# A message phase on one core: four buffers of compared places, four PSUM banks, a later turn for every engine, and a quarter of the filter loads on GpSimd's queue

## The reference

```python
xn = node @ Wn
f = ssp(edge @ We1 + be1)
f = f @ We2 + be2
msg = xn[edge_index[1]] * f                    # the message phase
agg = jax.ops.segment_sum(msg, edge_index[0], num_segments=N)
```

## Time and profile before

| | us |
|---|---|
| median of 3 runs | 5333.97 (5328.78 to 5336.42) |
| the profiled execution, device time | 5331.8 |
| its span from the first to the last instruction | 5329.5 |
| message phase in it, 1457 to 1983 | 526 |
| per turn of the phase, 526 / 208 | 2.53 |

### The profile page before, as it was taken

How to read it: one execution, slowest core, us unless ns; L and a number is a source line. 1 busy time by engine, 2 the same in 40 slices (tenths; PEclk the granted TensorE clock), 3 DMA queues, 4 the chain that set the end, 5 groups by cost and what they waited for, 6 DMA issues and landing times. The chain is left out here.

```text
span 5329.5 us, 53979 instructions
## 1 busy us (share of the span) xinstructions
PE 2753.4 (52%) x13381; PEld 2255.9 (42%) x13381; DVE 2761.4 (52%) x7383; ACT 1319.2 (25%) x3951; POOL 3381.0 (63%) x3625
## 2 busy tenths in 40 slices
PE   1477776777588884444444554334443244444445
PEld 1356555556456563333333443333333133333333
DVE  2699888888777763333333443333333533333334
ACT  4587666667366650000000110000000000000001
POOL 0677666767222237777777557777777377777773
PEclk8798989989676765555555665555555555555556
DMA  4666666667366652222222122222222322222224
GB/s 74 175 167 166 154 150 151 159 146 183 32 212 208 208 185 53 53 53 53 53 53 53 38 62 53 52 52 53 53 53 51 50 53 53 53 53 53 53 53 49
DMA packets 454220, 489.94 MB, mean 92 GB/s; under 512 B 86459, under 2 KB 359695, under 8 KB 453910
## 3 DMA queue, kind: packets, MB, share of 16 engines
q0 software_dynamic: 125248, 274.84, 22.2%
q1 hardware_dynamic: 325780, 210.91, 14.4%
q10 hardware_dynamic: 2882, 0.70, 0.1%
HBM read 359.63 MB, written 126.50 MB: 91 GB/s over the span
## 5 line engine op out<-in xcount | busy, mean ns | idle before, releaser
L1488 PE MATMUL bank<-arena 128*128 128x128 f32 x4992 | 1277.0, 437 | 1939.6 <-DVE arena L875 1706.3
L1488 PEld LDWEIGHTS bank<-arena 128*128 128x128 f32 x4992 | 1111.4, 328 | 2105.1 <-DVE arena L875 1863.8
L1562 POOL DMA_INDIRECT arena<-node_table,pick x1664 | 1579.1, 949 | 651.3 <-issue 506.9
L863 DVE TENSOR_TENSOR acc<-acc,bank 128x128 f32 x2496 | 720.0, 288 | 2070.8 <-PE bank L1488 1779.8
L1562 POOL DMA_INDIRECT arena<-gat_table,pick x832 | 853.5, 1026 | 361.0 <-issue 235.4
L1562 POOL DMA_INDIRECT arena<-message_table,pick x832 | 787.3, 946 | 255.8 <-issue 253.3
L1169 ACT COPY xt<-bank 128x512 f32<-128x512 f32 (+1 forms) x39 | 21.6, 555 | 2106.4 <-PE bank L1428 2106.4
L875 DVE TENSOR_TENSOR arena<-iota_free,local 128x512 f32<-128x512 f32 x624 | 427.9, 686 | 4.2 <-issue 2.8
L1477 PE MATMUL bank<-arena 128*128 x1664 | 350.7, 376 | 84.1 <-DVE arena L902 76.6
L1477 PEld LDWEIGHTS bank<-arena 128*128 128x128 f32 x1664 | 300.6, 271 | 160.6 <-issue 160.6
L1640 POOL DMA_DIRECT2D message_table<-arena x208 | 113.5, 546 | 393.2 <-DVE arena L902 393.2
(11 more groups left out here) (218 smaller groups left out, 3302.5 us busy)
## 6 DMA issues: line engine op xcount, KB each, us to landing
arena<-filter_table SPq DMA_DIRECT2D x832, 64.0 KB, 2.3
message_table<-arena POOLq DMA_DIRECT2D x208, 256.0 KB, 2.6
filter_table<-arena SPq DMA_DIRECT2D x196, 256.0 KB
xt<-edge_cols SPq DMA_DIRECT2D x131, 256.0 KB, 3.1
arena<-local_rows SPq DMA_DIRECT2D x208, 128.0 KB
arena<-node_table,pick POOLq DMA_INDIRECT x1664
arena<-edge_cols SPq DMA_DIRECT2D x65, 256.0 KB
arena<-gat_table,pick POOLq DMA_INDIRECT x832
```

The costliest lines, as they stand in the source:

```text
L863: e.tensor_tensor(a, a, bank[6 + t % 2][:, s * P:(s + 1) * P], ALU.add).then_inc(sums, 1)
L1488: ins = e.matmul(bank[6 + n % 2][:, s * P:(s + 1) * P], hot[n % 2][:, s, :], gathered[:, slot(n, s), 0:D], start=True, stop=True)
L1562: e.indirect_dma_start(out=dst, out_offset=None, in_=table, in_offset=bass.IndirectOffsetOnAxis(ap=index, axis=0)).then_inc(done, 16)
```

## The change

`hot_n` gets four buffers (`HN`). The spread node rows get four banks, 0, 1, 4 and 5 (`spread_bank`), in place of two. PE multiplies turn t-3 in its turn t, in place of t-1, and waits for `m_made` of turn n-4. DVE's turn t now begins with the product of turn t-4, then compares turn t-1, then adds the bias of turn t-3; the comparison of turn n waits for `m_spread` and `degree_added` of turn n-4. The fourth filter DMA of every turn (step `GRP - 1`) is issued by POOL, with its own registers, ahead of the message's write; SP issues three. DVE's addition waits for both.

```diff
-        hot_n = [part([P, GRP * P]) for _ in range(2)]
+        hot_n = [part([P, GRP * P]) for _ in range(HN)]          # HN = 4
...
+        def spread_bank(n):
+            return bank[(0, 1, 4, 5)[n % 4]]
...
-            for t in range(TICKS + 2):
-                n = t
-                if n < TICKS:
-                    e.wait_ge(m_places, n + 1)
-                    if n > 1:
-                        e.wait_ge(m_spread, n - 1)
-                        e.wait_ge(degree_added, (n - 1) * GRP)
-                    e.tensor_scalar(hot_n[n % 2][:, :], bank[2 + n % 2][:, :], iota_part[:, 0:1], None, ALU.is_equal
-                                    ).then_inc(m_hot, 1)
-                n = t - 1
-                if 0 <= n < TICKS:
-                    e.wait_ge(f_in[n % FT], f_value(n))
-                    filled[n] = own(e.tensor_tensor(filter_in[n % FT][:, :, :], filter_in[n % FT][:, :, :],
-                                                 filter_row[:, :].unsqueeze(1).to_broadcast([P, GRP, D]), ALU.add))
-                n = t - 2
+            for t in range(TICKS + 4):
+                n = t - 4
                 if n >= 0:
                     e.wait_ge(m_spread, n + 1)
                     after(filled[n])
                     if n >= MT:
                         e.wait_ge(m_out[n % MT], 16 * (n // MT))
-                    e.tensor_tensor(message[n % MT][:, :, :], bank[n % 2][:, :].rearrange("p (s d) -> p s d", s=GRP),
+                    e.tensor_tensor(message[n % MT][:, :, :], spread_bank(n)[:, :].rearrange("p (s d) -> p s d", s=GRP),
                                     filter_in[n % FT][:, :, :], ALU.mult).then_inc(m_made, 1)
+                n = t - 1
+                if 0 <= n < TICKS:
+                    e.wait_ge(m_places, n + 1)
+                    if n >= HN:
+                        e.wait_ge(m_spread, n - HN + 1)
+                        e.wait_ge(degree_added, (n - HN + 1) * GRP)
+                    e.tensor_scalar(hot_n[n % HN][:, :], bank[2 + n % 2][:, :], iota_part[:, 0:1], None, ALU.is_equal
+                                    ).then_inc(m_hot, 1)
+                n = t - 3
+                if 0 <= n < TICKS:
+                    e.wait_ge(f_in[n % FT], f_value(n))
+                    e.wait_ge(ring[n % RT], last_filter_value(n))
+                    filled[n] = own(e.tensor_tensor(filter_in[n % FT][:, :, :], filter_in[n % FT][:, :, :],
+                                                 filter_row[:, :].unsqueeze(1).to_broadcast([P, GRP, D]), ALU.add))
...
-            for t in range(TICKS + 1):                            # PE
+            for t in range(TICKS + 3):
...
-                n = t - 1
+                n = t - 3
...
                 e.wait_ge(m_hot, n + 1)
-                if n > 1:
-                    e.wait_ge(m_made, n - 1)
+                if n > 3:
+                    e.wait_ge(m_made, n - 3)
...
+            def last_filters_in(n):                               # POOL
+                if n % 4 == 0:
+                    e.load(starts, start_row[:, n * GRP:n * GRP + 16])
+                at = e.snap(starts[(n * GRP + GRP - 1) % 16], min_val=0, max_val=2 * EW - P)
+                e.dma_start(filter_in[n % FT][:, GRP - 1, :], filter_table[bass.ds(at, P), :]
+                            ).then_inc(ring[n % RT], 16)
+
             places_in(0)
             places_in(1)
-            for t in range(TICKS + 2):
+            for k in range(2):
+                e.wait_ge(f_out[k], 16 * FTICKS // 2)
+            e.wait_ge(start_in, 48)
+            e.wait_ge(summed, STEPS)
+            e.wait_ge(win_taken, 8)
+            for n in range(FT):
+                last_filters_in(n)
+            for t in range(TICKS + 4):
                 if t % LT == 2 and 1 < t // LT + 1 < TICKS // LT:
                     places_in(t // LT + 1)
-                n = t - 2
+                n = t - 4
                 if n >= 0:
                     e.wait_ge(m_made, n + 1)
+                    if n + FT < TICKS:
+                        last_filters_in(n + FT)
                     e.dma_start(messages[:, n * GRP:(n + 1) * GRP, :], message[n % MT][:, :, :]
...
-                for s in range(GRP):                              # SP
+                for s in range(GRP - 1):
```

More of the change, by code:

```diff
@@ L47 @@
 LT = 4
+HN = 4
 CHUNKS = -(-E // P)
@@ L351, in ring_value, with last_filter_value @@
         def ring_value(layer, t):
-            return 16 * GRP * (LAYERS[layer] * laps[t % RT] + t // RT + 1)
+            k = t % RT
+            return 16 * GRP * (LAYERS[layer] * laps[k] + t // RT + 1) + 16 * laps[k] * (layer != "gat")
+        def last_filter_value(n):
+            return 16 * (GRP * laps[n % RT] + n // RT + 1)
+        def spread_bank(n):
+            return bank[(0, 1, 4, 5)[n % 4]]
         def f_value(n):
             k = n % FT
-            return 16 * (len(range(k % 3, FTICKS if k < 3 else TICKS, 3)) + GRP * (n // FT + 1))
+            return 16 * (len(range(k % 3, FTICKS if k < 3 else TICKS, 3)) + (GRP - 1) * (n // FT + 1))
         def sum_place(t, s):
@@ L1191, in scalar @@
                         e.wait_ge(degree_added, i)
-                    e.activation(hot_copy[:, :], hot_n[n % 2][:, s * P:(s + 1) * P], ACT.Copy,
+                    e.activation(hot_copy[:, :], hot_n[n % HN][:, s * P:(s + 1) * P], ACT.Copy,
                                  accum_out=degree_part[:, i:i + 1]).then_inc(degree_added, 1)
@@ L1472, in tensor @@
                 e.wait_ge(m_hot, n + 1)
-                if n > 1:
-                    e.wait_ge(m_made, n - 1)
+                if n > 3:
+                    e.wait_ge(m_made, n - 3)
                 for s in range(GRP):
                     b = e.snap(blocks[(n * GRP + s) % 16], min_val=0, max_val=NB)
-                    ins = e.matmul(bank[n % 2][:, s * P:(s + 1) * P], hot_n[n % 2][:, s * P:(s + 1) * P],
+                    ins = e.matmul(spread_bank(n)[:, s * P:(s + 1) * P], hot_n[n % HN][:, s * P:(s + 1) * P],
                                    xn[:, bass.ds(b, 1), :].rearrange("p o d -> p (o d)"), start=True, stop=True)
@@ L1630, in places_in @@
                             ).then_inc(l_in[b % 2], 16)
+            starts = [e.register(f"start_reg_g{k}").__enter__() for k in range(16)]
+            def last_filters_in(n):
[4 more added lines that the diff above has]
+                            ).then_inc(ring[n % RT], 16)
             places_in(0)
             places_in(1)
-            for t in range(TICKS + 2):
+            for k in range(2):
[6 more added lines that the diff above has]
+            for t in range(TICKS + 4):
                 if t % LT == 2 and 1 < t // LT + 1 < TICKS // LT:
                     places_in(t // LT + 1)
-                n = t - 2
+                n = t - 4
                 if n >= 0:
                     e.wait_ge(m_made, n + 1)
+                    if n + FT < TICKS:
+                        last_filters_in(n + FT)
                     e.dma_start(messages[:, n * GRP:(n + 1) * GRP, :], message[n % MT][:, :, :]
```

## The result

The changed kernel takes 5297.3 us (5293.15 to 5312.49, four runs) against 5333.24 before: ratio 0.994, interval 0.9925 to 0.9955. It is faster by 36 us (0.6%) where I forecast 75. The profiled execution is the slowest of its four, 5312.49 us.

The account below looks back on a forecast made before the run. SP's filter issuing, 2.54 us a turn, was taken as the bound. Turns of 1.98 us (high clock, 0.6) and 2.54 (low) gave 2.17, a phase of 453 us, 73 shorter: 5259 us, 8 in 10 from 5215 to 5300.

Parts of the forecast that it names:

- What bounds the kernel now: Message phase: SP's issuing of four filter DMAs sets the pace, 2.54 us a turn; PE's low-clock turn is equally long.
- unbroken row: SP's timeline: 750 filter DMAs without a gap for 477.08 us, read as SP setting the pace.
- The 1.96: SP's queue: a turn with three filter issues, register load and slow issues included, takes 1.96 us.
- It joins POOL's queue: POOL's queue: a filter issue costs 0.73 us, making its turn 1.65; timing of places left at no change.
- Four banks and a later turn for PE: PE: its 72.3 us of waits for DVE's messages go; DVE's 58.7 us for places go only partly.
- DVE's order: DVE: the product directly behind the addition it waits for starts 0.72 us after it; turn grows from 1.86 to 1.98.
- my own shares: PE's clock in the phase: high level 0.6 of the time, low level 0.4.
- The clock: PE's clock: high-level share rises from 0.38 to 0.6, giving 2.17 us a turn and a phase of 453 us.
- my 8 in 10: Whole kernel: the time lies between 5215 and 5300 us.
- a slow POOL: Rival at POOL's queue: its turn of 2.17 us becomes the bound, 5286 us; chance 0.08.
- the clock doesn't improve: Rival at PE's clock: high share stays 0.38, phase 478, time 5284 us; 5335 if low throughout; chance 0.15.
- four buffers of compared places alone buy nothing: ACT's copies: ACT waits for DVE, not the reverse, so these buffers alone gain nothing.

Follow-up runs that it names:

- e1: The changed kernel with all four filter loads of a turn back on SP, its buffers, banks and later turns kept; ratio to before 0.9995.
- e7: The kernel before with only the fourth filter load on POOL and the places asked for one turn earlier; ratio to before 0.9945, on another chip.
- e9: The changed kernel with PE's register load moved, DVE's product last, a third places buffer and places asked a whole group ahead; 5227.22 us, ratio 0.9808.
- e2: The kernel before with only the fourth filter load of a turn issued by POOL; ratio to before 1.0017.
- e3: The changed kernel with PE's load of 16 registers moved behind the last matmuls of the four turns before; 5277.05 us, ratio 0.9895.
- e12: The changed kernel with PE's 16 block registers loaded only once, before the first turn; ratio to before 0.9901, on another chip.
- e4: The changed kernel with DVE's turn in the order comparison, bias, product; 5267.41 us, ratio 0.9882.
- e11: The changed kernel run again unchanged; ratio to before 0.9937, phase 484.9 us.
- e10: The changed kernel with one more float32 128x128 matmul in each turn of PE; ratio to before 0.9943, phase 487.0 us.
- e6: The changed kernel with PE's register load moved, DVE's product last and places asked one turn earlier; ratio to before 0.9844, on another chip.

## Where the prediction was right and where it was wrong

**What bounds the kernel now: right, though I leaned on the wrong row.** SP's 2.54 us a turn was the pace: e1 shows that nothing helps while SP issues four, e7 that taking one away is enough once the places are in time. The "unbroken row" of SP shows nothing by itself, since the timeline merges SP's issues across waits too (the changed kernel's 546, with 44 waits, are one row as well). What carried the argument was the 7.9 us of SP's waits. The 1.96 that I took for three issues a turn fits e9, where SP is nearly full: 2.02, and 1.95 without its waits.

**It joins POOL's queue: the sum right, its parts not, and one dependence missed.** The filter's issue took 0.53 us and not 0.73. The register load took 1.45 at the median (L1646) and not 0.98, which is 0.36 a turn. Together with 0.54 and 0.13 that makes 1.56 where I had 1.65, and POOL was no bound. The places were late for only 2.3 us, as I said. But I left their timing at no change after a rough count, and e2 shows how much hangs on it: in the kernel with two banks, two buffers and the old turns the same split made PE wait 61.1 us for them and cost the whole gain.

**Four banks and a later turn for PE: the step that failed.** I wrote that PE's 72.3 us of waits for `m_made` go, and put nothing in their place. The waits themselves did go: none of PE's stops ahead of its matmuls is left at a turn without a register load, where 59.1 of 76.6 us had been. But once in four turns PE loads 16 registers between a turn's places and its matmuls, and for that my sum had no term, though it had one for SP's and one for POOL's. Before, it hid in part under the other waits (17.5 us at turns with a load); with these gone it stops PE for 40.7 us in 34 stops, and 46.5 us in 40 with those that the view puts down to others. The view names a product that was made long ago. The load is worth 15 to 21 us moved (e3) and 24 to 30 removed (e12, on another chip) of the 32 to 37 by which the phase is longer than I said.

**DVE's order: seen, and mis-sized.** I had 1.98 for the turn, from 0.72 between addition and product; it was 2.04 and 0.78. With my own shares that is 0.6 / 2.04 + 0.4 / 2.54 = 0.452, a turn of 2.21 and a phase of 462, 9 us more, and close to the 460.4 of e12, where the load is gone. Undoing the order gave 30 to 35 us (e4), so a dependence that costs 0.18 us a turn cost more than its count. That DVE's floor also held PE back is my guess; no run takes it apart.

**The clock: over-estimated, and not the cause alone.** With the measured share and turn, 0.46 / 2.04 + 0.54 / 2.54 = 0.438, 2.28 a turn, 476 us; for e11, whose share is 0.50, it is 472. The 13 to 15 us left are turns longer than their level's, such as the one of 2.47 us around the load's stop (1702.87 to 1705.34). Whether the low share is a cause or follows from PE's stops is open: in e12 the mean clock rose to 0.77 with the load gone, in e4 to 0.79 with DVE's order, in e3 it stayed at 0.75 with the stop moved, while a clock raised by extra work (e10) gave nothing.

**The range and the rival: luck.** 5297 lies 3 us inside the upper end of my 8 in 10, which I had drawn past a slower clock and a slow POOL and not for this. The case "the clock doesn't improve" came near the time (5284 with a share of 0.38), but the share did improve, to 0.46, and the rest came from PE's stops.

**Right besides.** Turns at the low level are 2.54 us (matmuls from 1449.69, 1452.23 and 1454.77), the first product comes 1 us later behind the first comparison (4.9 us for 3.9), filters are never late, and four buffers of compared places alone buy nothing, as far as e1 can show it. The gathers of messages are unchanged; those of the last two layers were 13 to 14 us longer in two profiles, which nothing here explains.

## What to carry to other kernels

When a queue that sets the pace is relieved, list what becomes the next one by name and price, including instructions that no busy time shows: here a register load of 1.15 us, once in four turns, was worth half of the missing gain or more. A wait that is put down to an engine which finished long ago points at such an instruction: count the stops by turn, and see if they fall where the instruction is. A row of a queue that the timeline draws without a gap doesn't show that the queue is full; its own waits do. And a transfer that is just in time must be timed anew with every change around it: asking for it one turn earlier was, beside the split, worth as much as four banks, four buffers and the new turns.

## What the runs showed of the hardware

PE's TENSOR_LOAD of 16 registers took 1.10 to 1.83 us in the changed kernel, and the matmuls behind it began 0.18 to 0.47 us after its end, in all 52 cases. Matmuls issued ahead of it go on: in e3 one load ran from 1567.00 to 1569.13 while eight of them ran from 1567.08 to 1569.16. Moved behind eight of them it left one stop of 0.9 us ahead of the matmuls that need it (e3). At the high clock those eight last 1.16 us and the load 1.92 at the median (e6), and PE then stopped 16.5 us ahead of the next spread. SP's loads of this kind went from 0.98 us at the median before to 1.38 in the changed kernel, where POOL loads registers too (1.45); why isn't shown.

A DVE operation that waits for the one before it started 0.78 us after the start of that one, which takes 0.68; one that doesn't wait started 0.60 after, while it still ran.

SP's issue of a 64 KB load took 0.525 us in a clean row. Over long stretches, with register loads and waits, it was 0.636 on the mean (208 GB/s, before) and 0.672 (261 GB/s, e9), so a queue's floor isn't the clean row's. POOL's issue of the same load, with an address from a register, took 0.53 us.
